# Layer-3 attention's first keys and queries prepared one stage earlier, its row scores first, three dense products before and in its first batch, and the output stored by chunk

## The chip, the cores and the metric

The kernel runs on one core of a Trainium2 chip. The metric is the device time of one execution in microseconds, and lower is better. Three runs of the kernel before took 2995.62, 2998.90 and 3001.24 us, so the median is 2998.9 us.

## The reference

A network of four layers works on 16 sequences of 256 tokens with 128 features, all in float32. Each layer is a macaron: half a feed-forward network, attention, and half of the same feed-forward network again, each on the layer norm of x and added to x. The change touches layer 3 alone:

```python
x = x + 0.5 * ffn(layernorm(x));  x = x + attn(layernorm(x));  x = x + 0.5 * ffn(layernorm(x))

def attn(x, W_q, W_k, W_v, W_o):             # 16 heads of 8 features
    q, k, v = heads(x @ W_q.T), heads(x @ W_k.T), heads(x @ W_v.T)
    s = einsum('bhqd,bhkd->bhqk', q, k) / sqrt(8)
    return merge(einsum('bhqk,bhkd->bhqd', softmax(s), v)) @ W_o.T

def ffn(x, ...):                             # 128 -> 512 -> 512 -> 512 -> 128
    h = silu(lin(x, w1)) * lin(x, w2)
    h = gelu(lin(h, h1));  h = gelu(lin(h, h2))
    return lin(h, w3)
```

## The kernel before, in words

The program is a row of stages, one after the other, with a barrier of all engines at the start of each (`Stage.ready`). x stays in SBUF throughout, in `fields`, as 32 tiles of 128 tokens. A chunk is 4 tiles (`CT`), that is 512 tokens (`CW`) or two sequences, and there are 8 chunks. Each stage has a program for SP (which issues DMAs in order), GpSimd, VectorE, ScalarE and TensorE, and each engine runs its program strictly in order; semaphores tie them together. `sig.past(n)` is the count that a signal has after its n-th event, plus the credit that it starts with. The layer norm has helpers: `ln_scales_dve` (L143 to 155) forms mean and variance from sums kept with x, `ln_scales_pool` (L161) takes the power, `ln_dve` (L180) normalises a chunk into `xn`, `ln_pe` (L190) transposes it into the one PSUM bank `tp`, and `ln_act` (L196) copies that to `xnt`. `new_sums_dve` (L203) forms the sums of a new chunk of x.

`l3_ffn` runs twice, with first=True ahead of the attention and first=False behind it. In each chunk (`body`) TensorE makes eight products of the hidden layer (L2834); ScalarE takes silu (L2767) and VectorE multiplies (L2746). Then come two layers h1 and h2 (`layer`), each in seven products of half size (L2788) instead of eight, by a scheme of sums and differences: VectorE forms the sums t1 to t4 (L2713 to 2721) and combines each product from its PSUM bank as soon as it is there (L2724 to 2738), ScalarE copies the first product (L2772) and takes gelu (L2775). In the end TensorE makes the output product (L2847), VectorE adds it to x (L2752) and forms the new sums (L203). Chunks 0 to 5 run in a hardware loop; chunks 6 and 7 are written out, and c is a Python integer there. SP has no program in this stage.

`l3_attn` handles a batch (one sequence) in 16 steps of two heads each. The scores are computed twice. `row_scores` (L3205) gives queries by keys, of which VectorE takes the maximum of each row (`largest`, L3052). The maxima are split into three bfloat16 parts (`split_maxima`, L3057 to 3063), transposed (`turn_maxima`, L3212), copied (`keep_nm`, L3137) and put by three small DMAs (`place_nm`, L2975) into three extra rows of the query tile `qx`. `key_scores` (L3221) then gives keys by queries with the maximum already taken off, ScalarE takes the exponential (L3133), and `values` (L3233) multiplies with V. Row scores run ahead: 16 steps of batch 0 and `LEAD` = 8 steps of batch 1 come ahead of the main loop, and the loop makes those of later batches between its own steps. The main loop's first instruction on TensorE is a row-score step that waits for `nm_moved`.

Keys and queries are float32 values held as three bfloat16 parts each, laid out in 72 rows (`kx`, `qx`), which are filled through DRAM. For each chunk TensorE makes two projections (`project`, L3191), ScalarE copies them to `proj` (`keep`, L3128), a split makes the three parts, SP stores them to `k_dram` and `q_dram` (`store`, L2954 and 2957) and loads them once per batch in the order that the scores need (`load`, L2965 and 2968: one transfer of 576 KB and three of 192 KB). For chunks 0 and 1 VectorE makes the split in the stage's start (L3034 to 3040), for the others GpSimd in the loop (L3018 to 3024). Order at the stage's start, on each queue:

- SP: four weight loads (L2946), the ones (L2979), store(0,0), load(0,0,0), load(0,0,1), store(1,1), load(1,1,0), place_nm(0,0,0).
- TensorE: four weight transposes (L3261), `ln_pe` 0, K and Q projection of chunk 0, `ln_pe` 1, K and Q projection of chunk 1, V projection of chunk 0 (L3195), 16 row-score steps of batch 0, 8 of batch 1 with the transposes of the maxima behind the second, main loop.
- VectorE: constants (L3080 to 3082), layer-norm scales, `ln_dve` 0 and 1, four splits, the copy of V (`keep_v`, L3045), 16 maxima, `split_maxima`, 8 maxima, main loop.
- ScalarE: four weight copies (L3151, L3153), then for each of two chunks `ln_act` and two `keep`, `keep_nm`, main loop.

The last stage, `end`, waits at its barrier and stores all of x with one DMA (L3399).

## Time and profile before

| | |
|---|---|
| Median of three runs | 2998.9 us |
| The profiled execution's own time | 3000.47 us |
| Its span | 2998.3 us |
| Mean granted clock of TensorE | 0.851 of full speed |
| Layer-3 feed-forward, first run of it | 2076 to 2365 us of the span |
| Layer-3 attention | 2367 to 2698 us |
| Layer-3 feed-forward, second run of it | 2699 to 2989 us |
| Output | 2989.5 to 2998.3 us |

The profile shows one execution. Engines are PE (TensorE's matmuls), PEld (its weight loads, which overlap them), DVE (VectorE), ACT (ScalarE), POOL (GpSimd) and SP. L12 is line 12 of the kernel. In the timeline each line has the start, the duration of the whole group, the engine, the line, the operation, output<-inputs, the count, and in brackets the engine's idle time before it with what ended it. The table of stretches gives, for each stretch of the span, its length, then busy time and count of PE, PEld, DVE, ACT and POOL in this order, PEclk, the DMA engines' share and GB/s. PEclk is the TensorE clock that the throttle granted, as a share of full speed: 1.00 is 2.4 GHz, 0.50 is 1.2 GHz. Ends of matmuls are modelled, so a busy PE is not necessarily PE at its peak. A float32 product of 512 columns is two matmul instructions.

### The profile page before, as it was taken

Reading aid. Unit: us, or ns where it says so; the run is one execution under the profiler, and the core shown is the slowest. Engines: PE = TensorE matmul, PEld = TensorE weight load, DVE = VectorE, ACT = ScalarE, POOL = GpSimd, SP = SyncE. Lnnn points to the kernel's source line nnn. Section 1 sums busy time; section 2 is a strip of 40 time slices with the busy share of each in tenths; the row PEclk is TensorE's granted clock in tenths of the full one; section 3 lists DMA queues with packets and bytes.
Section 4 is the critical chain, followed back from the end, with each engine's and each line's share of the span. In section 5 each row is a group of like instructions: output and inputs, shape, how many; then the busy total and the mean of one; then the engine's idle time right before and its main releaser. Section 6 shows DMA issues by size and latency. Waiting matters only on the chain. (4 is left out here: it accounts for less than half of the span.)

```text
span 2998.3 us, 46339 instructions
## 1 busy us (share of the span) xinstructions
PE 2306.7 (77%) x14088; PEld 1668.0 (56%) x14089; DVE 1753.8 (58%) x4313; ACT 1064.7 (36%) x2478; POOL 850.1 (28%) x770
## 2 busy tenths in 40 slices
PE   4979959767376740675999982575999799989998
PEld 3645546447354720563666651464888545547877
DVE  5758957563576359821343348833565578765565
ACT  1433324431144110453444422353333246663332
POOL 2535425437313730673000010574000112201000
PEclk9989959865596555897999986798999779999999
DMA  6110011336514675454000017364000133310000
GB/s 207 39 59 1 1 40 41 101 139 143 144 34 153 144 211 71 92 119 117 1 1 0 1 40 143 77 122 99 1 0 0 36 96 89 87 43 1 0 0 29
DMA packets 274629, 204.04 MB, mean 68 GB/s; under 512 B 102432, under 2 KB 253453, under 8 KB 271405
## 3 DMA queue, kind: packets, MB, share of 16 engines
q1 hardware_dynamic: 240301, 168.05, 20.2%
q0 software_dynamic: 34176, 34.09, 7.0%
q8 instruction: 79, 1.29, 0.2%
q14 instruction: 73, 0.60, 0.1%
HBM read 136.20 MB, written 64.91 MB: 67 GB/s over the span
## 5 line engine op out<-in xcount | busy, mean ns | idle before, releaser
L161 POOL TENSOR_TENSOR fields<-ln_t,power 128x4 f32<-128x4 f32 x96 | 98.3, 1050 | 590.9 <-DVE ln_t L154 590.9
L3052 DVE TENSOR_REDUCE s_mx<-s_sa 128x2 f32<-128x512 f32 x256 | 166.2, 686 | 57.8 <-PE s_sa L3205 56.7
L3133 ACT ACTIVATE s_e<-s_sc 128x512 f32<-128x512 f32 x256 | 149.7, 600 | 99.6 <-PE s_sc L3221 96.7
L2788 PE MATMUL s_z<-s_t,s_mix_h 128*128 128x256 f32 x768 | 171.0, 379 | 0.0
L1996 POOL DMA_INDIRECT acc_dram<-s_yo,s_to_i x96 | 152.4, 1588 | 45.8 <-issue 27.0
L1984 POOL DMA_INDIRECT s_xg<-rows_dram,s_from_i x96 | 94.6, 985 | 223.0 <-DVE s_to_i L2117 195.0
L2788 PEld LDWEIGHTS s_z<-s_t,s_mix_h 128*128 128x128 f32 x768 | 146.0, 190 | 19.7
L190 PE MATMUL s_tp<-ident,xn 128*128 128x128 f32 x224 | 46.4, 344 | 133.8 <-DVE xn L180 132.0
L2406 DVE TENSOR_SCALAR s_den<-s_kn 128x8 f32<-128x8 f32 x64 | 10.3, 161 | 209.0 <-PE s_kn L2567 209.0
L3205 PE MATMUL s_sa<-s_kx,s_qx 72*128 72x256 bf16 x512 | 109.4, 300 | 27.1 <-DMA s_qx<-q_dram 15.0
L2301 PE MATMUL s_hu<-s_xgt,s_w 128*128 128x128 f32 x768 | 118.1, 300 | 7.9 <-issue 6.0
L2834 PE MATMUL s_z<-xnt,s_wt_w 128*128 128x512 f32 x256 | 116.8, 610 | 1.5 <-ACT xnt L196 1.5
L190 PEld LDWEIGHTS s_tp<-ident,xn 128*128 128x128 f32 x224 | 34.2, 183 | 147.5 <-DVE xn L180 133.7
L2396 POOL TENSOR_TENSOR s_rd<-s_rv,s_power 128x2 f32<-128x2 f32 x16 | 11.1, 697 | 369.5 <-DVE s_rv L2430 369.5
L1251 POOL DMA_INDIRECT acc_dram<-s_yo,s_to_i x64 | 101.7, 1588 | 30.6 <-issue 17.6
L2206 ACT ACTIVATE s_h<-s_hu,s_b 128x128 f32<-128x128 f32 x384 | 109.1, 375 | 1.2 <-PE s_hu L2301 1.2
L2301 PEld LDWEIGHTS s_hu<-s_xgt,s_w 128*128 128x128 f32 x768 | 99.3, 202 | 15.4 <-issue 9.4
L425 POOL DMA_INDIRECT y_dram<-s_xg,s_to_ids x78 | 76.7, 983 | 109.6 <-DVE s_xg L583 109.6
L2311 PE MATMUL s_lp<-s_w,s_h 128*128 128x128 f32 x768 | 106.2, 283 | 1.8 <-ACT s_h L2206 1.7
L3221 PE MATMUL s_sc<-s_qx,s_kx 75*128 75x256 bf16 x512 | 103.0, 285 | 0.9 <-DMA s_qx<-s_nm 0.5
L415 POOL DMA_INDIRECT s_xg<-x_dram,s_ids x78 | 75.5, 968 | 99.2 <-DVE s_ids L548 72.5
L2311 PEld LDWEIGHTS s_lp<-s_w,s_h 128*128 128x128 f32 x768 | 96.4, 197 | 3.5 <-ACT s_h L2206 3.5
(516 smaller groups left out, 6105.0 us busy)
## 6 DMA issues: line engine op xcount, KB each, us to landing
s_w<-in_L_ffn_W_dram SPq DMA_DIRECT2D x96, 256.0 KB, 3.0
acc_dram<-s_zero SPq DMA_DIRECT2D x32, 512.0 KB, 5.8
s_kx<-k_dram SPq DMA_DIRECT2D x16, 576.0 KB
s_qx<-q_dram SPq DMA_DIRECT2D x48, 192.0 KB
fields<-acc_dram SPq DMA_DIRECT2D x16, 512.0 KB, 7.5
table_dram<-s_table_rows SPq DMA_DIRECT2D x2, 3136.0 KB, 9.2
s_wg<-in_L_ffn_w_gate_dram SPq DMA_DIRECT2D x64, 96.0 KB, 2.1
s_wu<-in_L_ffn_w_up_dram SPq DMA_DIRECT2D x64, 96.0 KB, 2.2
```

The source lines that it names most:

```text
L161: pool.tensor_tensor(core.rstd[:, tiles], core.ln_t[:, 2, tiles], core.power[:, 0:CT], ALU.pow).then_inc(s.scale_ready.sem, 1)
L1251: pool.indirect_dma_start(sums, bass.IndirectOffsetOnAxis(ap=to_i[:, n:n + 1], axis=0), yo[:, n % RING, :], None, compute_op=ALU.add).then ...
L1996: pool.indirect_dma_start(sums, bass.IndirectOffsetOnAxis(ap=to_i[:, n:n + 1], axis=0), yo[:, n % RING, :], None, compute_op=ALU.add).then ...
L2206: last = act.activation(h[:, u, j, :], hu[:, u, j * P:(j + 1) * P], ACT.Gelu, bias=b1[:, j, n:n + 1])
L2301: last = pe.matmul(hu[:, u, j * P:(j + 1) * P], w1[:, n % RING, j, :], xgt[:, u, :], start=True, stop=True)
L2311: pe.matmul(lp[:, u, j * P:(j + 1) * P], h[:, u, j, :], w2_flat[:, first:first + P], start=j == 0, stop=False)
L2788: last = pe.matmul(bank(n)[:, o, :], weights[:, f, o * P:(o + 1) * P], src[:, f, :], start=f == 0, stop=f == HALF - 1)
L2834: pe.matmul(z[:, (2 * f + half) % 4, :], wt[m][:, 0, f * P:(f + 1) * P], core.xnt[:, u, :], start=True, stop=True).then_inc(up_done.sem, 1)
L3052: dve.tensor_reduce(mx[:, i, t, 2 * pairs:2 * pairs + 2], sa[:, n % 2, :, :], AX.X, ALU.max).then_inc(max_done.sem, 1)
L3133: act.activation(e[:, n % RING, :, :], sc[:, n % 2, :, :], ACT.Exp).then_inc(exp_done.sem, 1)
L3205: last = pe.matmul(sa[:, n % 2, a, :], qx[0:ROWS, slot, h, t * P:(t + 1) * P], kx[0:ROWS, slot, h, :], start=True, stop=True)
L3221: last = pe.matmul(sc[:, n % 2, a, :], kx[:, slot, h + a, k * P:(k + 1) * P], qx[:, slot, h + a, :], start=True, stop=True)
```

## The change

In `l3_ffn` with first=True, chunks 6 and 7 also prepare keys and queries of chunks 0 and 1 for the attention (a = 0 in chunk 6, a = 1 in chunk 7): layer norm from x, transposes, two projections, three parts and their stores. The helper `early(c, k, at)` on each engine is called at places inside `layer`, where k is the layer and `at` the place. The work area is `all_xn`, free in this stage, and the bank `tp`. In `l3_attn` SP begins with the load of batch 0, and TensorE with its row scores; weight transposes, `ln_pe` and the V projection stand between row-score steps 10 and 15. `keep_v` stands behind `split_maxima`. `warm()` is a product of 512 columns whose result nobody reads, twice ahead of the main loop and once at step 1 of batch 0. In the last stage each chunk of x is stored as soon as it is added up, and the sums L203 are left out there. The stage `end` is gone.

```diff
@@ l3_ffn, SP @@
+        if first:
+            @block.sync
+            def _(sp):
+                for n, m in enumerate(("W_k", "W_q")):
+                    sp.dma_start(raw_a[n], w[f"L3_attn_{m}"]).then_inc(aw_loaded.sem, 16)
+                for a in range(EARLY):
+                    for n in range(2):
+                        sp.wait_ge(a_split_done.sem, a_split_done.past(2 * a + n))
+                        for i in range(2):
...
+                                sp.dma_start(core.k_dram[2 * a + i].rearrange("a d h t -> (d h) a t"), cut).then_inc(a_stored[0].sem, 16)
+                            else:
+                                for k in range(TERMS):
+                                    sp.dma_start(core.q_dram[2 * a + i, :, k, :, :], cut[:, k, :]).then_inc(a_stored[1].sem, 16)
+                sp.wait_ge(a_stored[0].sem, 32 * EARLY)
+                sp.wait_ge(a_stored[1].sem, 32 * TERMS * EARLY)
+        if not first:
...
+                for c in range(CHUNKS):
+                    tiles = slice(c * CT, (c + 1) * CT)
+                    sp.wait_ge(x_added.sem, x_added.past(c))
+                    sp.dma_start(out_rows[:, tiles, :], core.x[:, tiles, :]).then_inc(out_stored.sem, 16)
+                sp.wait_ge(out_stored.sem, 16 * CHUNKS)
@@ l3_ffn, VectorE @@
+            def early_left(a, n):
+                dve.wait_ge(a_first_cut.sem, a_first_cut.past(2 * a + n))
+                dve.scalar_tensor_tensor(left[n], s.tp[:, 0, :], SCALE if n else 1.0, parts[:, n, 0, :],
+                                         ALU.mult, ALU.subtract).then_inc(a_left_ready.sem, 1)
+            def early_last(a, n):
+                dve.wait_ge(a_second_cut.sem, a_second_cut.past(2 * a + n))
+                dve.tensor_tensor(parts[:, n, 2, :], left[n], parts[:, n, 1, :], ALU.subtract).then_inc(a_split_done.sem, 1)
+            def early(c, k, at):
...
+                if a == 0 and k == 0:
+                    if at == 0:
+                        early_scales()
+                    if at == 3:
+                        early_normal(0, range(2))
+                    if at == 4:
+                        early_normal(0, range(2, CT))
+                if (a, k) in ((0, 1), (1, 0)):
+                    if at == 2:
+                        early_left(a, 0)
+                    if at == 4:
+                        early_last(a, 0)
+                    if at == 5:
+                        early_left(a, 1)
+                if a == 0 and k == 1 and at == 6:
+                    early_last(0, 1)
+                if a == 1 and k == 1 and at == 0:
+                    early_last(1, 1)
...
             def body(c, u, more=True):
                 if more:
                     ln_dve(dve, core, s, c + 1, 1 - u)
+                elif first:
+                    early_normal(1)
...
-                dve.wait_ge(x_added.sem, x_added.past(c))
-                new_sums_dve(dve, core, c)
+                if first:
+                    dve.wait_ge(x_added.sem, x_added.past(c))
+                    new_sums_dve(dve, core, c)
@@ l3_ffn, ScalarE @@
+            def early_cut(a, n):
+                act.wait_ge(a_projected.sem, a_projected.past(2 * a + n))
+                if a:
+                    act.wait_ge(a_stored[n].sem, (32, 32 * TERMS)[n] * a)
+                act.activation(parts[:, n, 0, :], s.tp[:, 0, :], ACT.Copy, scale=SCALE if n else 1.0).then_inc(a_first_cut.sem, 1)
+            def early_cut2(a, n):
+                act.wait_ge(a_left_ready.sem, a_left_ready.past(2 * a + n))
+                act.activation(parts[:, n, 1, :], left[n], ACT.Copy).then_inc(a_second_cut.sem, 1)
...
+                if (a, k) in ((0, 1), (1, 0)):
+                    if at == 1:
+                        early_cut(a, 0)
+                    if at == 2:
+                        early_cut2(a, 0)
+                    if at == 3:
+                        early_cut(a, 1)
+                    if at == 4:
+                        early_cut2(a, 1)
@@ l3_ffn, TensorE @@
+            def early_project(a, n):
+                if n:
+                    pe.wait_ge(a_left_ready.sem, a_left_ready.past(2 * a))
+                else:
+                    pe.wait_ge(a_xnt_ready.sem, a_xnt_ready.past(a))
+                pe.matmul(s.tp[:, 0, :], wt_a[n], xta, start=True, stop=True).then_inc(a_projected.sem, 1)
...
                 product(held.quarter(m, 0, 1), b21, 1)
+                early(c, k, 1)
...
                 product(s2, t2, 4)
+                early(c, k, 2)
...
                 product(held.quarter(m, 1, 1), t4, 0)
+                early(c, k, 5)
                 pe.wait_ge(taken.sem, taken.past(now))
                 product(s4, b22, 1)
+                early(c, k, 6)
@@ l3_attn, SP @@
-            for m in names:
-                sp.dma_start(raw[m][:, :], w[f"L3_attn_{m}"]).then_inc(w_loaded.sem, 16)
...
+            load(0, 0, 0, False)
+            for m in names:
+                sp.dma_start(raw[m][:, :], w[f"L3_attn_{m}"]).then_inc(w_loaded.sem, 16)
+            load(0, 0, 1, False)
             sp.wait_ge(ones_ready.sem, 1)
...
-            store(0, 0)
-            load(0, 0, 0, False)
-            load(0, 0, 1, False)
-            store(1, 1)
             load(1, 1, 0, False)
             place_nm(0, 0, 0)
@@ l3_attn, VectorE @@
-            dve.memset(ones[:, :], 1.0).then_inc(ones_ready.sem, 1)
-            dve.memset(m3[:, :, :, TERMS:, :], 0.0)
-            dve.tensor_copy(ident_b[:, :], core.ident[:, :]).then_inc(ident_ready.sem, 1)
             ln_scales_dve(dve, core, s)
             ln_dve(dve, core, s, 0, 0)
             ln_dve(dve, core, s, 1, 1)
-            split(0, 0)
-            split(0, 1)
-            split(1, 0)
-            split(1, 1)
-            dve.wait_ge(v_clear.sem, 2)
-            keep_v(0, 0)
+            dve.memset(ones[:, :], 1.0).then_inc(ones_ready.sem, 1)
+            dve.memset(m3[:, :, :, TERMS:, :], 0.0)
+            dve.tensor_copy(ident_b[:, :], core.ident[:, :]).then_inc(ident_ready.sem, 1)
             for n in range(STEPS):
                 largest(0, 0, n)
             split_maxima(0)
+            dve.wait_ge(v_clear.sem, 2)
+            keep_v(0, 0)
@@ l3_attn, TensorE @@
+            def warm():
+                pe.matmul(pj[:, :], wt["W_v"][:, :], core.xnt[:, 0, :], start=True, stop=True)
...
             pe.wait_ge(kq_loaded[0].sem, 64)
             for n in range(STEPS):
                 row_scores(0, 0, n)
+                if n == T_FIRST:
+                    pe.wait_ge(w_loaded.sem, 16 * len(names))
...
+                if n == T_FIRST + 1:
+                    ln_pe(pe, core, s, 0, 0)
+                if n == T_FIRST + 3:
+                    ln_pe(pe, core, s, 1, 1)
+                if n == T_FIRST + 4:
+                    pe.wait_ge(w_kept.sem, 1)
+                    project_v(0, 0)
...
+            pe.wait_ge(v_kept.sem, v_kept.past(0))
+            warm()
+            warm()
             pe.wait_ge(ones_loaded.sem, 16)
-            pe.wait_ge(v_kept.sem, v_kept.past(0))
...
                             turn_maxima(b + 1, 1 - i)
+                        if n == 1 and not prev:
+                            warm()
                         key_scores(b, slot, n)
```

T_FIRST is 10. The credits of `pj_kept` and `parts_stored` are raised by what chunks 0 and 1 gave before, and the counts that wait for them shift by 2 * EARLY.

## Rows read from the trace of the kernel before

**Rows 1.** The table of stretches: length, busy time of each engine, PEclk, DMA share, GB/s.

```profile
2298.00:2334.00 36.00, 36.00 (x167) 28.59 (x166) 20.38 (x34) 12.26 (x18) 0.00 (x0) 1.00 0.00 1
...
2371.00:2399.00 28.00, 12.58 (x28) 5.48 (x27) 14.22 (x25) 4.37 (x10) 10.09 (x10) 0.50 0.35 88
...
2406.00:2424.00 18.00, 13.23 (x50) 4.84 (x50) 13.35 (x27) 3.58 (x6) 0.00 (x0) 0.50 0.62 151
...
2424.00:2440.00 16.00, 16.00 (x94) 7.13 (x94) 8.07 (x15) 7.48 (x14) 0.00 (x0) 0.50 0.01 3
...
2456.00:2488.00 32.00, 30.43 (x294) 17.69 (x286) 25.33 (x60) 21.48 (x41) 8.74 (x8) 1.00 0.40 96
...
2610.00:2620.00 10.00, 10.00 (x73) 5.08 (x71) 5.75 (x11) 5.96 (x12) 2.40 (x3) 0.80 0.17 25
...
2704.00:2716.00 12.00, 11.51 (x28) 5.93 (x29) 3.77 (x6) 4.63 (x7) 4.37 (x5) 0.77 0.00 1
```

**Rows 2.** Timeline of the attention stage's start: start us, us, engine, line, operation [idle before].

```profile
2366.94 0.34 SPq L2946 DMA_DIRECT2D s_raw_W_q<-in_L_attn_W_q_dram  x1
...
2371.25 1.12 PE L190 MATMUL s_tp<-ident,xn 128*128 128x128 f32 x4
...
2385.16 2.07 PE L3195 MATMUL s_pj<-s_wt_W_v,xnt 128*128 128x128 f32 x8 [0.69 <-ACT s_proj L3128]
...
2389.58 0.80 SPq L2965 DMA_DIRECT2D s_kx<-k_dram  x1
...
2391.97 0.88 DVE L3045 COPY s_vz<-s_pj 128x128 f32<-128x128 f32 x4
...
2398.94 1.04 PE L3205 MATMUL s_sa<-s_kx,s_qx 72*128 72x256 bf16 x4 [11.71 <-DMA s_qx<-q_dram]
```

**Rows 3.** Timeline of the first maxima and the loop's start.

```profile
2399.59 11.04 DVE L3052 TENSOR_REDUCE s_mx<-s_sa 128x2 f32<-128x512 f32 x16 [6.74 <-PE s_sa L3205]
...
2411.62 5.46 DVE L3052 TENSOR_REDUCE s_mx<-s_sa 128x2 f32<-128x512 f32 x8
...
2412.60 2.60 SPq L2975 DMA_DIRECT2D s_qx<-s_nm  x3
...
2419.29 0.59 PE L3205 MATMUL s_sa<-s_kx,s_qx 72*128 72x256 bf16 x2 [2.94 <-DMA s_qx<-s_nm]
```

**Rows 4.** End of the program on the timeline; transfers' sizes and time to landing.

```profile
2987.33 0.69 DVE L2752 TENSOR_TENSOR fields<-fields,s_y 128x512 f32<-128x512 f32 x1 [2.93 <-PE s_y L2847]
...
2988.05 0.87 DVE L203 BATCH_NORM_STATS2 fields<-fields 128x6 f32<-128x128 f32 x4
...
out_dram<-fields SPq DMA_DIRECT2D x1, 2048.0 KB, 8.4
...
s_raw_W_q<-in_L_attn_W_q_dram SPq DMA_DIRECT2D x1, 64.0 KB, 1.8
```

**Rows 5.** Timeline of the first feed-forward stage, chunks 6 and 7.

```profile
2308.35 0.69 DVE L2729 TENSOR_TENSOR s_u<-s_u,s_z 128x512 f32<-128x512 f32 x1 [1.04 <-PE s_z L2788]
...
2329.03 7.03 PE L2834 MATMUL s_z<-xnt,s_wt_w 128*128 128x512 f32 x16
```

**Rows 6.** Timeline of the first batch: value products and the first K projection.

```profile
2426.86 1.08 PE L3233 MATMUL s_ob<-s_e,s_vz 128*32 128x256 f32 x8
...
2429.70 1.08 PE L3233 MATMUL s_ob<-s_e,s_vz 128*32 128x256 f32 x8
...
2439.82 1.92 PE L3191 MATMUL s_pj<-xnt,s_wt_W_k 128*128 128x512 f32 x2
...
2442.95 0.76 PE L3233 MATMUL s_ob<-s_e,s_vz 128*32 128x256 f32 x8
```

**Rows 7.** Timeline of later batches: value products, and a wait for a load.

```profile
2493.13 0.64 PE L3233 MATMUL s_ob<-s_e,s_vz 128*32 128x256 f32 x8
...
2494.68 0.64 PE L3233 MATMUL s_ob<-s_e,s_vz 128*32 128x256 f32 x8
...
2606.04 0.39 PE L3205 MATMUL s_sa<-s_kx,s_qx 72*128 72x256 bf16 x2 [1.96 <-DMA s_qx<-q_dram]
```

More of the change, by code:

```diff
@@ L2689, in _ @@
             ln_scales_pool(pool, core, s)
+            if first:
+                pool.wait_ge(a_var_ready.sem, 1)
+                for c in range(EARLY):
+                    tiles = slice(c * CT, (c + 1) * CT)
+                    pool.tensor_tensor(core.rstd[:, tiles], core.ln_t[:, 2, tiles], core.power[:, 0:CT],
+                                       ALU.pow).then_inc(a_scale_ready.sem, 1)
         @block.vector
@@ L2704, in _, with early_scales @@
                     dve.tensor_tensor(s4, a12, s2, ALU.subtract).then_inc(mixed.sem, 1)
+            def early_scales():
+                tiles = slice(0, EARLY * CT)
+                me, mo = core.sums[:, tiles, 1], core.sums[:, tiles, 4]
+                t0, t1, t2 = (core.ln_t[:, i, tiles] for i in range(3))
+                dve.tensor_tensor(t0, me, mo, ALU.add)
+                dve.tensor_tensor(t1, me, mo, ALU.subtract)
+                dve.tensor_tensor(t2, core.sums[:, tiles, 2], core.sums[:, tiles, 5], ALU.add)
+                dve.drain()
+                dve.tensor_scalar(core.mean[:, tiles], t0, 0.5, None, ALU.mult)
+                dve.tensor_tensor(t1, t1, t1, ALU.mult)
+                dve.tensor_scalar(t2, t2, 1.0 / D, 1e-5, ALU.mult, ALU.add)
+                dve.drain()
+                dve.scalar_tensor_tensor(t2, t1, 0.25, t2, ALU.mult, ALU.add).then_inc(a_var_ready.sem, 1)
@@ new lines, in early_normal @@
+            def early_normal(a, tiles=range(CT)):
+                dve.wait_ge(a_scale_ready.sem, a_scale_ready.past(a))
+                if a:
+                    dve.wait_ge(a_turned.sem, a_turned.past(a - 1))
+                for j in tiles:
+                    t = a * CT + j
+                    last = dve.tensor_scalar(xa[:, j, :], core.x[:, t, :], core.mean[:, t:t + 1], core.rstd[:, t:t + 1],
+                                             ALU.subtract, ALU.mult)
+                if CT - 1 in tiles:
+                    last.then_inc(a_xn_ready.sem, 1)
@@ L3422, in build @@
             l3_ffn(core, held, False)
-        end(core)
 def kernel(**inputs):
```

161 lines of the change are left out of this document (108 added, 53 removed).

## The prediction

> **What bounds the kernel now.** I read the stages first, in the table of stretches. In the first Layer-3 feed-forward stage TensorE is busy 36.00 of 36 us at the full clock, VectorE 20.4 and ScalarE 12.3 [rows 1]: every product put there lengthens it, vector and scalar work need not. The start of the attention stage is the opposite: TensorE is busy 12.58 of 28 us from 2371 to 2399, and its granted clock is 0.50, the 1.2 GHz level, from there through 2440, even in 2424 to 2440 where it is busy 16.00 of 16 us. The same loop later runs at 1.00 [rows 1].
>
> The timeline then says what the start waits for. The first DMA is issued at 2366.94; call that t = 0. Weights, projections, splits in three parts, the store to DRAM and the load back follow each other; the load is issued at t = 22.6 and the first row scores run at t = 32.0, after 11.71 us idle for that DMA [rows 2]. Then VectorE sets the pace: 16 maxima take 11.04 us, 8 more 5.46 us, and the main loop begins at 2419.29, t = 52.35, behind the three transfers of the maxima [rows 3]. At the end of the program the last addition starts at 2987.33; the sums for a layer norm that nobody reads, a barrier and one 2048 KB store, 8.4 us to landing, are all exposed [rows 4].
>
> **The change, part by part.** Durations are those of one execution: 3000.47 us, span 2998.3 us, 2.2 us around it. The median of the runs shown is 2998.9, 1.6 us lower; I subtract my sum from the median as well.
>
> *Early keys and queries, in the feed-forward stage.* TensorE gets four projections of 512 columns, two matmuls each: 16 such matmuls take 7.03 us [rows 5], so 0.88 us each and 3.5 us. It gets 10 transposes; four took 1.12 us at the half clock [rows 2], so 0.14 us each at full clock and 1.4 us. That is 4.9 us on a full engine; I take **+5.0**. VectorE gets eight normalisations, four subtractions and four last parts of 0.69 us, and seven small operations for the scales, about 9 us over some 60 us; ScalarE eight cuts and four copies, about 7 us; GpSimd two small powers. Cover: VectorE idles 1.04 us ahead of most reads of a product [rows 5] and 2.93 us ahead of the last addition [rows 4], and the added pieces are put behind such reads one at a time. The tightest place is the end of the first layer of chunk 7: one 0.69 us subtraction stands ahead of the next layer's first sum, about the slack that the third product there leaves. If instead each of the four projections exposed its copy and its subtraction (0.6 + 0.69 us), the cost would be 10; the floor is 3.5, projections alone. SP, empty in this stage before, issues two weight loads and 16 stores. The last ones are released early in chunk 7's second layer, with most of a layer and the output products still to run, more than the 9.4 us that a whole load took [rows 2]; they should not hold the barrier.
>
> *Row scores first.* SP now issues load(0,0,0) at t = 0, ahead of the four weight loads, the other loads, the ones and the maxima. The transfer that let scores start 9.36 us after its issue [rows 2] does so at t = 9.4. Bounds: 7.5, if the second load behind it took some of the bandwidth; 12, if the weights and two more loads disturb it more. Its cover is gone, for nothing else is ready: PE waits for it alone. The 16 maxima take 11.7 us from there (2398.94 to 2410.63). Between steps 10 and 14 PE now does the four weight transposes, two turns of xn and the V projection: 1.1 + 1.1 + 1.1 + 2.07 us at the half clock [rows 2]. PE needs 0.43 us for a step where VectorE needs 0.69 and runs at most two steps ahead; followed step by step, VectorE starves for 0.2, 0.8 and 2.4 us, so +3.4 (bounds 1 and 5.4). Maxima done: t = 24.5. Splitting them takes 1.0 us (2410.63 to 2411.62), the V copy that now stands behind it 0.9 [rows 2], the 8 maxima of the next batch 5.5; PE's last row scores need the sixth of them and end at t = 31.1. The transfers of the maxima start at t = 26.4 and take 2.6 us to issue; before, the scores waited 4.1 us beyond that [rows 3], with a load issued just ahead in the same queue. Now the loads stand long before them; with the 1.8 us of a small transfer [rows 4] they land at 30.8, at worst 33.1. Two dense products at the half clock, 1.76 us each (twice 0.88), end at t = 34.6 and cover both. So the loop starts at 34.6 and not at 52.35: **-17.8** (bounds -14 and -21).
>
> *Three dense products.* The first 16 steps took 23.66 us, 2419.29 to 2442.95; two steps take 2.84 us at the half clock, 1.55 at the full one [rows 6, 7]. Eight pairs at 1.55, the norm transposes and one K projection give about 14; the 16 maxima with their normalisation want 12.9 on VectorE; I take 15. So a full clock from the first step is worth 8.7. Against it, the third product costs 0.9 to 1.0 in the loop, and I allow 1.2 for a rise inside the first pairs. **-6.5**, bounds +1.8 (no rise) and -8.
>
> That the clock rises is the uncertain step. In 2424 to 2440 a busy engine stayed at 0.50, and the next short durations stand right behind the 1.92 us K projection of 2439.82 [rows 1, 6]; the next feed-forward stage starts cold with such products and has a mean of 0.77 within 12 us [rows 1]. Dense products raise it, row and key scores alone did not. But single projections with pauses, 2371 to 2399, did not either. The Trainium skill ("TensorE: Matmul & The Clock Gate", Part 1) says that sustained matmul activity releases the throttle and an idle stretch brings it back. By that rule 2424 to 2440 should have been fast, and the three products would be a mere cost, with the time of rival (a); the trace disagrees with it, 16.00 us busy at 0.50.
>
> *Output by chunk.* Seven stores of 256 KB land beside chunks 1 to 7. The last follows the last addition, done at 2988.02. Between 64 KB in 1.8 us and 2048 KB in 8.4 us [rows 4] lies 2.4 for 256 KB; with 0.15 of wake and the 0.36 that the span had after landing it ends at 2990.9 for 2998.3: **-7.3** (bounds -6.5 and -7.7). The sums that go with it cost nothing in the other chunks, where TensorE is full.
>
> Sum: 5.0 - 17.8 - 6.5 - 7.3 = -26.6. The profiled execution would be 2973.9, the median **2972**.
>
> **Rivals.** (a) *The clock does not rise before the first K projection.* For it: the cold projections with pauses, and scores that hold nothing up. The third product costs 1.8 and nothing comes back: 5.0 - 17.8 + 1.8 - 7.3 = -18.3, time 2981. (b) *The faster loop start runs into the loads.* The loop has such a wait: 1.96 us for a load at 2606.04, and a clock of 0.80 in the ten microseconds after it [rows 1, 7], some 4 us together. If the ring of stores and loads, now entered sooner, makes two more of these, 2980. Against it: later rounds already run at this pace. (c) *The feed-forward stage loses its clock.* The new handshakes are the first pauses that TensorE would have in chunks 6 and 7. Where they bring 1.2 GHz, the work takes twice as long: x us of full-clock work cost x. It decides from about 33 of the 72 us on (26.6 gained, 6 of margin); the whole second chunk, 36 us, gives 3008. Against it: each projection waits for work that is finished a product earlier, and the clock was 1.00 throughout.
>
> **Numbers.** Forecast 0.63, with 2966 to 2977 as its own range; (a) 0.20; (b) 0.11; (c) 0.06. The range reaches over (a) and (b) with the bounds of the load: 2963 to 2984. A measurement of this kernel tells about 0.2%, 6 us, from no change. Forecast, (a) and (b) are all beyond it; of (c) most is slower, some cancels, and a late load together with (a) could come near: faster 0.92, same 0.03, slower 0.05.
>
> **What would show it.** Feed-forward chunks 6 and 7 some 2.5 us longer each, clock 1.00; first row scores 9 to 10 us after the stage's first DMA; the loop's first step near t = 35; the first eight pairs at 1.5 to 2 us each; the end 3 us behind the last addition. The forecast is wrong if the granted clock of the first batch stays at 0.50, if the first load lands after t = 12, or if the feed-forward chunks grow by more than 5 us each.

## The result and the profile after

| | before | changed |
|---|---|---|
| Median, same comparison | 3000.07 us (6 executions, 2995.62 to 3011.46) | 2966.11 us (6 executions, 2959.86 to 2969.40) |
| Ratio | | 0.9878, interval [0.9859, 0.9896] |
| Span of the profiled execution | 2998.3 us | 2965.7 us |
| Mean granted clock | 0.851 | 0.858 |

The changed kernel is 34.0 us faster by the medians. The forecast was 26.6 us less, 2972 with a range of 2963 to 2984. A second set of six executions gave 2972.80 us for the same kernel; all twelve together have a median of 2968.5.

The table of stretches of the changed kernel, columns as in [rows 1], around the places that those rows show of before:

```profile
2301.00:2337.00 36.00, 36.00 (x173) 28.84 (x171) 24.12 (x47) 14.44 (x24) 1.99 (x2) 1.00 0.05 14
2371.00:2399.00 28.00, 13.75 (x70) 8.11 (x68) 15.32 (x39) 1.98 (x6) 11.73 (x11) 0.63 0.62 127
2399.00:2409.00 10.00, 6.83 (x28) 2.76 (x27) 7.21 (x18) 1.67 (x2) 0.00 (x0) 0.83 0.50 120
2408.40:2424.00 15.60, 15.09 (x136) 8.05 (x135) 12.06 (x25) 10.35 (x20) 0.13 (x1) 1.00 0.15 34
2424.00:2440.00 16.00, 15.57 (x152) 9.09 (x149) 13.44 (x31) 11.21 (x22) 8.60 (x8) 1.00 0.19 52
2456.00:2488.00 32.00, 31.05 (x302) 18.07 (x300) 25.97 (x61) 22.48 (x43) 8.74 (x8) 1.00 0.40 101
...
2610.00:2620.00 10.00, 8.92 (x93) 5.43 (x91) 7.98 (x19) 6.84 (x14) 0.00 (x0) 1.00 0.77 183
```

The feed-forward stage still has a full TensorE at the full clock, with four more microseconds of VectorE in 36. Ahead of the main loop the clock still has means of 0.62 and 0.83. From the loop's start, 2408.40, it is 1.00, where the loop before began at 0.50 and stayed there through 2440 [rows 1].

The timeline of the attention stage's start in the changed kernel (start us, us, engine, line, operation, idle time before), against [rows 2, 3, 6]:

```profile
2375.90 0.84 SPq L3170 DMA_DIRECT2D s_kx<-k_dram  x1
2376.79 1.34 SPq L3173 DMA_DIRECT2D s_qx<-q_dram  x3
...
2385.83 1.03 PE L3393 MATMUL s_sa<-s_kx,s_qx 72*128 72x256 bf16 x4 [13.14 <-DMA s_qx<-q_dram]
2386.47 7.66 DVE L3245 TENSOR_REDUCE s_mx<-s_sa 128x2 f32<-128x512 f32 x11 [5.34 <-PE s_sa L3393]
...
2394.47 1.06 PE L190 MATMUL s_tp<-ident,xn 128*128 128x128 f32 x4
...
2397.62 1.08 PE L3383 MATMUL s_pj<-s_wt_W_v,xnt 128*128 128x128 f32 x8
...
2401.50 1.87 SPq L3180 DMA_DIRECT2D s_qx<-s_nm  x3
...
2405.55 3.05 PE L3398 MATMUL s_pj<-xnt,s_wt_W_v 128*128 128x512 f32 x4
2408.44 0.38 PE L3393 MATMUL s_sa<-s_kx,s_qx 72*128 72x256 bf16 x2
...
2409.10 1.02 PE L3398 MATMUL s_pj<-xnt,s_wt_W_v 128*128 128x512 f32 x2
...
2411.90 0.64 PE L3424 MATMUL s_ob<-s_e,s_vz 128*32 128x256 f32 x8
```

Counted from the stage's first DMA, at 2375.90, the row scores begin at t = 9.9 (32.0 before) and the loop at t = 32.5 (52.35 before). The first value burst takes 0.64 us, where those of the first batch took 1.08 [rows 6].

The end of the changed kernel on its timeline, against [rows 4]:

```profile
2962.08 0.69 DVE L2876 TENSOR_TENSOR fields<-fields,s_y 128x512 f32<-128x512 f32 x1 [2.93 <-PE s_y L3053]
2962.79 0.37 SPq L2737 DMA_DIRECT2D out_dram<-fields  x1
```

and the store in the list of DMA issues on its page (size, us to landing):

```profile
out_dram<-fields SPq DMA_DIRECT2D x8, 256.0 KB, 2.3
```

**Where the time went.** I put the same marks on every profile. The *feed-forward* part runs from the stage's first layer-norm operation (L146 in the kernel before) to its last addition. *Load* runs from the attention stage's first DMA to the first row scores, *maxima* from there to the first operation of `split_maxima`, and *wait* from there to the loop's first step. *First batch* runs to the seventh value burst (2442.95 in [rows 6]), and *rest* from there to the attention's last addition to x. *End* runs from the program's last addition to the end of the span.

| kernel | feed-forward | load | maxima | wait | first batch | rest | end | span |
|---|---|---|---|---|---|---|---|---|
| before | 287.36 | 32.00 | 11.79 | 8.56 | 23.66 | 254.09 | 10.97 | 2998.3 |
| changed | 293.10 | 9.93 | 13.91 | 8.70 | 14.50 | 248.65 | 3.62 | 2965.7 |

Between these two executions the differences are +5.74 in the feed-forward stage, -19.81 in load, maxima and wait, -9.16 in the first batch, -5.44 in the rest and -7.35 at the end. The code ahead of the stage, which is the same, took 3.09 us more (2079.62 for 2076.53 us), and the gaps between the stages and the last feed-forward stage differ by 0.33 together. The sum is -32.6, the difference of the spans. Two of these entries are not the change's: the 3.09 and, as the experiments show, the 5.44.

Part of the 5.74 isn't either. The feed-forward stage starts at the lower clock in every profile, and for how long differs. Its first 16 us in the kernel before and in the changed one:

```profile
2076.50:2092.50 16.00, 11.68 (x33) 6.38 (x34) 12.12 (x29) 4.87 (x7) 9.80 (x8) 0.74 0.01 2
...
2079.60:2095.60 16.00, 11.69 (x27) 5.71 (x28) 11.04 (x27) 4.56 (x7) 9.80 (x8) 0.66 0.04 10
```

I take 16 times what PEclk lacks to 1.00 in these first 16 us off the length of the stage (before: 287.36 - 16 * 0.26 = 283.2; changed: 293.10 - 16 * 0.34 = 287.7). What is left is 283.1 to 283.2 us in the three profiles with the old stage and 287.6 to 287.8 in the ten with the new one and single projections. So the early keys and queries cost 4.5 us there, and 1.3 of the 5.74 are the clock at the stage's start.

### The profile page after: what moved, and what is told of

It reads as the page before. It is cut to its first block and busy times, and to the rows that moved or that the text cites. A ratio compares the mean times of both kernels' runs of the same rounds, so it can differ in the third digit from the quotient of the medians.

```text
span 2965.7 us, 46268 instructions
## 1 busy us (share of the span) xinstructions
PE 2292.0 (77%) x14104; PEld 1665.7 (56%) x14105; DVE 1740.3 (59%) x4288; ACT 1068.0 (36%) x2486; POOL 852.3 (29%) x772
## 3 DMA queue, kind: packets, MB, share of 16 engines
q8 instruction: 80, 1.31, 0.2%
## 5 line engine op out<-in xcount | busy, mean ns | idle before, releaser
L3393 PE MATMUL s_sa<-s_kx,s_qx 72*128 72x256 bf16 x512 | 102.5, 284 | 24.9 <-DMA s_qx<-q_dram 14.2
L196 ACT ACTIVATE xnt<-s_tp 128x512 f32<-128x512 f32 x56 | 33.5, 598 | 186.6 <-PE s_tp L190 186.6
```

The lines of the kernel that those rows point to most:

```text
L3393: last = pe.matmul(sa[:, n % 2, a, :], qx[0:ROWS, slot, h, t * P:(t + 1) * P], kx[0:ROWS, slot, h, :], start=True, stop=True)
```

## The experiments

Twelve kernels ran, in three sets of four, each set with its own executions of before: median 2998.84 us (14 executions) for before_again, before_dense, no_dense and no_third; 3001.25 (11) for after_again, one_store, double_projection and load_alone; 3000.46 (11) for no_two, queries_first, early_load and both. A gain below is the difference to the median of the same set. The table holds the marks of each kernel's one profiled execution; *start to loop* is load, maxima and wait together. *Clock loss* is a sum over the rest of the loop: it is cut into stretches of 8 us (the last 10 us or more left out), and each adds 8 times what its PEclk lacks to 1.00. The last column has TensorE's waits of 1.0 us or more for a DMA in that part.

| kernel | median | gain | feed-forward | load | start to loop | first batch | rest | clock loss | end | waits for a DMA |
|---|---|---|---|---|---|---|---|---|---|---|
| before | 3000.07 | | 287.36 | 32.00 | 52.35 | 23.66 | 254.09 | 5.3 | 10.97 | 1.12, 1.96, 1.13 |
| before_again | 2996.90 | | 288.49 | 33.10 | 54.12 | 23.52 | 249.05 | 0.0 | 11.90 | 1.13 |
| before_dense | 2990.76 | 8.1 | 287.60 | 33.02 | 53.70 | 14.49 | 259.22 | 8.6 | 10.95 | 1.96, 1.07, 1.32 |
| changed | 2966.11 | 34.0 | 293.10 | 9.93 | 32.54 | 14.50 | 248.65 | 0.0 | 3.62 | 1.08 |
| after_again | 2972.80 | 28.5 | 292.92 | 9.51 | 33.16 | 15.21 | 260.45 | 12.0 | 3.69 | 1.31, 1.72, 1.02 |
| no_dense | 2974.85 | 24.0 | 292.16 | 9.56 | 29.48 | 22.90 | 256.83 | 8.6 | 3.60 | 1.02, 1.47, 1.39 |
| no_two | 2962.64 | 37.8 | 291.85 | 9.83 | 29.48 | 16.45 | 247.61 | 0.0 | 3.68 | none |
| no_third | 2972.25 | 26.6 | 292.71 | 9.70 | 32.20 | 14.49 | 252.77 | 3.4 | 3.64 | 1.38, 1.18 |
| one_store | 2979.62 | 21.6 | 292.97 | 9.82 | 32.41 | 14.48 | 258.14 | 11.9 | 11.18 | 1.01, 1.53 |
| double_projection | 2971.37 | 29.9 | 296.53 | 9.33 | 32.57 | 14.50 | 252.73 | 3.4 | 3.66 | 3.40 |
| load_alone | 2970.39 | 30.9 | 292.31 | 9.34 | 34.54 | 15.86 | 257.60 | 10.2 | 3.71 | 1.06, 1.85 |
| queries_first | 2967.96 | 32.5 | 292.62 | 9.13 | 32.84 | 15.24 | 254.73 | 6.9 | 3.29 | 1.60, 1.56 |
| early_load | 2962.41 | 38.1 | 293.37 | 0.23 | 26.70 | 15.25 | 254.28 | 5.1 | 3.35 | 1.16, 1.09, 2.01 |
| both | 2975.29 | 25.2 | 293.23 | 0.23 | 26.63 | 15.20 | 253.05 | 5.1 | 3.75 | 1.32, 1.45 |

### The kernel before, once more

No edit. Expected:

> The kernel before, unchanged, for a second trace. Disputed is the stretch of the attention loop behind its first batch: 254.1 us in the first trace of before, 248.6 us in the trace of the changed kernel, which the prediction had at no difference. Theory A (the waits for loads and the low clock after them come and go from one execution to the next): this trace gives something other than 254, about 249 to 255, and its waits for the loads fall in other places. Theory B (the faster start removes them): 254 again, with the same wait near the middle of the loop, within 0.5 us.

One execution, 2996.9 us. The rest of its loop took 249.05 us, not 254.09. So the 5.44 us that the changed kernel seemed to save there lie within what one kernel does from one execution to the next.

### The dense products, all and one at a time

no_dense takes all three out; no_third takes out the one inside the loop, no_two the pair ahead of it; before_dense puts all three into the kernel before. Nobody reads these products, so leaving them out changes nothing that is computed.

```diff
-            warm()
-            warm()
...
-                        if n == 1 and not prev:
-                            warm()
```

> The changed kernel without its three dense products. Theory A (they bring the full clock to the first batch): the loop's first step comes some 2.7 us earlier, held by the row scores instead of the products, the first batch takes 22 to 24 us at a granted clock near 0.5 where the changed kernel takes 14.5 us, and the whole is 5 to 7 us slower than the changed kernel, about 2972. Theory B (the work now put between the row scores, above all the V projection during which the clock rose in the changed kernel's trace, does it alone): the first batch stays near 14 us and the whole is 3 us faster, about 2963.

> The changed kernel without the third dense product, the one at step 1 of batch 0. Theory A (two are enough, the third is a cost): first batch 0.9 us shorter at the full clock, the whole 0 to 1 us faster. Theory B (the clock falls again without it): first batch 20 us or more in some or all executions, the whole up to 8 us slower.

> The kernel before with nothing but the three dense products, at the same places. Theory A (they act by themselves): they end about 0.6 us later than the maxima's transfers, the first batch takes about 14.5 us instead of 23.7, and the whole is 8 to 9 us faster than before. Theory B (they act only together with the denser row scores of the changed kernel): the first batch stays near 23 us and the whole is 1 to 2 us slower than before.

> The changed kernel without the two dense products ahead of the loop; the one behind the first row scores of the next chunk, inside the loop, stays (nobody reads any of them). If it is these two that bring the clock back for the loop's first scores: the first seven value bursts take about 22.9 us, as with all three taken out, instead of 14.5, or somewhat less if the third product, some 10 us into the loop, raises the clock there (then about 18), and the prologue is some 3 us shorter, so that the kernel is 3 to 6 us slower than the changed one. If the clock would have risen by the work of the stage anyway: 14.5 us for the first bursts and 3 us faster than the changed kernel.

The stretch of no_dense that holds its first batch, in the columns of [rows 1]:

```profile
2404.00:2427.00 23.00, 22.75 (x121) 10.90 (x121) 12.64 (x25) 9.73 (x18) 0.00 (x0) 0.52 0.19 49
```

and that of before_dense:

```profile
2421.30:2435.90 14.60, 14.02 (x126) 7.50 (x126) 11.44 (x24) 9.31 (x18) 0.00 (x0) 1.00 0.26 57
```

With no dense product TensorE is busy 22.75 of 23 us and stays at the lower level, although the early keys and queries, the early load and all else of the change are there. With the products alone, in the kernel before, the first batch takes 14.49 us at 1.00 and the kernel gains 8.1 us (ratio 0.9970, interval [0.9957, 0.9983]). So the products are what raises the clock for the first batch, with the old start and with the new one.

no_third has the same first batch as the changed kernel, 14.49 us for 14.50: once the clock is up, the third product costs nothing. TensorE has room for it there: without it it is busy 13.40 of the 14.60 us. The medians can't confirm so small an effect: no_third has 2972.25 us, 3.8 above the changed kernel's twelve executions, and its six spread from 2965.16 to 2978.36. no_two shows that the third product isn't idle where it stands alone. Its timeline at the loop's start (TensorE only):

```profile
2398.63 0.58 PE L3393 MATMUL s_sa<-s_kx,s_qx 72*128 72x256 bf16 x2
2399.01 0.63 PE L3412 MATMUL s_sc<-s_qx,s_kx 75*128 75x256 bf16 x2
2399.43 0.63 PE L3393 MATMUL s_sa<-s_kx,s_qx 72*128 72x256 bf16 x2
2399.86 1.91 PE L3398 MATMUL s_pj<-xnt,s_wt_W_v 128*128 128x512 f32 x2
...
2402.42 1.04 PE L190 MATMUL s_tp<-ident,xn 128*128 128x128 f32 x4
2403.27 0.40 PE L3412 MATMUL s_sc<-s_qx,s_kx 75*128 75x256 bf16 x2
...
2404.05 0.64 PE L3424 MATMUL s_ob<-s_e,s_vz 128*32 128x256 f32 x8
```

Key scores of 0.63 us before the product have become 0.40 at 2403.27, 1.5 us behind its end. Without the pair the loop starts earlier, t = 29.48 for 32.54 (29.48 in no_dense too), and the first batch takes 16.45 us. From the first DMA to the seventh burst that is 45.93 us, for 47.04 with all three, 46.69 with the pair alone and 52.38 with none. The one product inside the loop does all that the three do, and the pair's own price, 3.1 us of the start, is saved. My expectation that no_two would be 3 to 6 us slower was wrong: a first batch of 18 us, which it allowed for, and a start 3 us shorter come to 0.5 us slower, and not to 3 to 6.

### The changed kernel, once more

No edit; in the set with the next three.

> The changed kernel, unchanged, again, as the measure for the three others and for the loop behind the first batch, which has taken 248.6 to 259.2 us in six traces whatever the kernel. Theory A (that stretch varies by waits for loads and low clock behind them, which no part of the change steers): 2966 again within 3 us, the stretch anywhere in 248 to 260, all other marks within 0.7 us of the first trace. Theory B (the changed kernel is steadily free of these waits): the stretch 248 to 249 again.

All marks up to the loop lie within 0.7 us of the first profile, and the first batch takes 0.7 us more. The clock rose later there, some 2 us into the loop. The loop's first 3 us:

```profile
2408.30:2411.30 3.00, 3.00 (x14) 1.83 (x13) 2.31 (x6) 0.65 (x2) 0.00 (x0) 0.66 0.58 109
```

Of the ten profiles with the pair, five have first batches of 14.48 to 14.50 us; in the other five (after_again, load_alone, queries_first, early_load, both) the first 3 us have a mean of 0.51 to 0.66, and the batch takes 15.20 to 15.86.

The rest of the loop differs far more: 260.45 us for 248.65, with a span of 2978.3. The median of 2972.80 lies outside the 3 us around 2966 that I had expected. The table of stretches:

```profile
2520.30:2536.30 16.00, 15.03 (x110) 7.92 (x111) 9.21 (x17) 8.70 (x17) 3.43 (x4) 0.79 0.35 65
2536.30:2544.30 8.00, 7.53 (x75) 5.17 (x74) 7.05 (x20) 4.55 (x10) 5.32 (x5) 1.00 0.23 65
2544.30:2562.30 18.00, 16.77 (x123) 8.97 (x120) 11.25 (x25) 9.55 (x18) 0.00 (x0) 0.72 0.57 135
```

and its timeline at the two waits behind which the first losses of this loop stand, from 2442 (outside the stretches shown) and from 2521:

```profile
2442.02 0.39 PE L3393 MATMUL s_sa<-s_kx,s_qx 72*128 72x256 bf16 x2 [1.31 <-DMA s_qx<-s_nm]
...
2521.27 0.39 PE L3393 MATMUL s_sa<-s_kx,s_qx 72*128 72x256 bf16 x2 [1.72 <-DMA s_qx<-q_dram]
```

TensorE waits 1.3 or 1.7 us for a transfer, and a stretch below the full clock follows: 16 us at 0.79 behind the second wait, which are 3.4 us lost. This is the pattern of rival (b).

### One store at the end

The changed kernel with the old `end` stage and its sums; the feed-forward stage stores nothing.

```diff
-                    sp.wait_ge(x_added.sem, x_added.past(c))
-                    sp.dma_start(out_rows[:, tiles, :], core.x[:, tiles, :]).then_inc(out_stored.sem, 16)
...
+            sp.dma_start(core.out.rearrange("b (n p) d -> p (b n) d", p=P), core.x[:, :, :]).then_inc(out_stored.sem, 16)
+            sp.wait_ge(out_stored.sem, 16)
```

> The changed kernel with the output stored as before: one store of all of x in a stage of its own, and the sums formed again in the last stage. Theory A (the part acts at the end alone): from the last addition to the end 11.0 us and not 3.6, everything else the same, the whole 7.3 us slower than the changed kernel. Theory B (stores and missing sums also act within the stage): the last feed-forward stage itself differs from 288.4 us by over 0.5 us.

Its end, on the timeline:

```profile
2967.62 0.69 DVE L2864 TENSOR_TENSOR fields<-fields,s_y 128x512 f32<-128x512 f32 x1 [2.93 <-PE s_y L3040]
2968.35 0.87 DVE L203 BATCH_NORM_STATS2 fields<-fields 128x6 f32<-128x128 f32 x4
...
2969.83 0.41 SPq L3577 DMA_DIRECT2D out_dram<-fields  x1
```

11.18 us for 3.69 in after_again, so 7.5 us; the medians differ by 6.8 (2979.62 for 2972.80). The feed-forward stage of the end keeps its length, 288.7 us for 288.5: the seven stores beside it are free, and the sums that fell away there give nothing back.

### Each early projection twice

```diff
+                pe.matmul(s.tp[:, 0, :], wt_a[n], xta, start=True, stop=True)
                 pe.matmul(s.tp[:, 0, :], wt_a[n], xta, start=True, stop=True).then_inc(a_projected.sem, 1)
```

> The changed kernel with each of the four early projections made twice into the same place. Theory A (TensorE is full there, so that all it gets is paid): four more products of 512 columns, 0.86 us each, make the first Layer-3 feed-forward stage 3.4 us longer, 293.1 to 296.5. Theory B (part of the 5.7 us that the stage grew is waiting between engines, and TensorE has room there): it grows by less than 2 us. The whole 3.4 us slower, or 0 to 2.

The first product of each pair does the same work once more. The stage took 296.53 us, 291.1 without the clock's loss in its first 16 us (PEclk 0.66), where the ten profiles with single projections have 287.6 to 287.8. So four more projections cost 3.4 us, 0.86 each, which is TensorE's own time for them: TensorE is the limit there. The median doesn't show it, 2971.37 us for 2972.80 in after_again; the scatter of the executions is larger.

### The first load alone in the queue

SP waits for the first load before it issues anything else.

```diff
             load(0, 0, 0, False)
+            sp.wait_ge(kq_loaded[0].sem, 64)
             for m in names:
```

> The changed kernel, with SP waiting for the load of batch 0 to land before it issues the weights, the second load, the ones and the third load. Theory A (the first load shares the DMA engines with what is issued behind it): it lands after some 7.5 us and not 9.9, the loop starts 2.4 us earlier, since the weights (2 us) and the second load are still in time for steps 10 and 16, and the whole is 2 us faster. Theory B (the first load is served in order and has the engines to itself already): it lands at 9.5 to 9.9 again and nothing gains; if the second load then comes late, up to 2 us slower.

The first scores began 9.34 us after the first DMA, alone in the queue, and 9.13 to 9.93 us in the eight profiles with the other loads behind it. Those loads take nothing from it that this scatter would let one see. The Trainium skill ("DMA: Bandwidth & Descriptors", the section "Queues, rings and completion order") says that each DMA engine takes the descriptors of one queue in order; the 9.34 against 9.13 to 9.93 agrees.

What was held back came late, and the loop began at t = 34.54 for 32.54. The row scores of the second batch waited only 0.34 us for their load. The loop's first step waited longer, TensorE idle for 2.57 us behind the pair:

```profile
2407.31 3.00 PE L3399 MATMUL s_pj<-xnt,s_wt_W_v 128*128 128x512 f32 x4
2412.88 0.53 PE L3394 MATMUL s_sa<-s_kx,s_qx 72*128 72x256 bf16 x2 [2.57 <-issue]
```

The profile names no cause for that idle time, but this step waits for the three transfers of the maxima, issued from 2403.26 on, and the view of the tile `s_nm` has for them

```profile
DMA to landing us min/median/max: 4.2/4.5/8.2
```

for 1.9/1.9/2.0 in no_third. The last was issued at 2404.54, so it landed at about 2412.8. Why it took 8.2 us is open.

### Queries ahead of keys in the loop

In the loop the queries are projected, split, stored and loaded ahead of the keys, and their load is issued ahead of the transfers of the maxima.

```diff
-                pe.matmul(pj[:, :], wt["W_q" if n else "W_k"][:, :], core.xnt[:, u, :], start=True, stop=True).then_inc(projected.sem, 1)
+                pe.matmul(pj[:, :], wt["W_k" if n else "W_q"][:, :], core.xnt[:, u, :], start=True, stop=True).then_inc(projected.sem, 1)
...
                     store(c + 2, u)
+                    load_q(c + 2, u, 0)
                 if after:
                     place_nm(2 * c + 2, 2 * (1 - u), 0)
                 if after > 1:
-                    load(c + 2, u, 0)
+                    load_k(c + 2, u, 0)
```

> The changed kernel with the queries projected, split and stored before the keys, and the load of the queries issued ahead of the transfers of the row maxima, that of the keys behind them. My theory: in the loop the row scores of a new slot wait for the queries' load, by 0.3 to 3.4 us, and the rest of the attention loop is 248.7 us in an execution without a late one and up to 260.5 us with late ones and the stretches at 0.5 clock that follow. If so, the waits of TensorE for the queries' load are gone or under 0.3 us each, the rest of the loop stands at 248 to 252 us, and the median is about 4 us under the changed kernel's, 2966 us by the one or 2964 by the other. First rival: the waits move to the keys' load, now last, and nothing is gained (within 2 us of the changed kernel). Second rival: the transfers of the row maxima now stand behind the queries' load and come late, so that the scores of the next chunk wait for them: slower by 1 us or more for each chunk, 5 us and up in all.

The summed waits of TensorE in the loop of queries_first (us in total, times, the longest):

```profile
PE s_sa L3401 <- DVE s_mx L3253: 4.4, 15, 0.5
PE s_sa L3401 <- DMA s_qx<-s_nm: 4.4, 5, 1.6
```

and of the changed kernel:

```profile
PE s_sa L3393 <- DVE s_mx L3245: 4.4, 15, 0.5
PE s_sa L3393 <- DMA s_qx<-s_nm: 2.2, 3, 0.8
PE s_sa L3393 <- DMA s_qx<-q_dram: 1.1, 1, 1.1
```

The waits for the load of queries are gone, as expected, but those for the transfers of the maxima became longer, 1.60 and 1.56 us, and each stands ahead of a stretch below 1.00. The rest was 254.73 us, outside the expected 248 to 252; the median, 2967.96, is the changed kernel's (2968.5 over its twelve executions). What happened is the second rival's mechanism, the transfers of the maxima late behind the queries' load, at a smaller price than its 5 us and up. The three longest waits for these transfers in the loops of all fourteen profiles are those of the two kernels with this order (1.60 and 1.56 here, 1.45 in both). The keys' load, the first rival's candidate, appears in no wait.

### The first load one stage earlier, and both

early_load gives the first batch's keys and queries tiles of their own and loads them while the feed-forward stage still runs. The attention stage begins with row scores.

```diff
@@ l3_ffn, SP, behind the stores of a = 0 @@
+                        sp.wait_ge(a_stored[0].sem, 32)
+                        sp.wait_ge(a_stored[1].sem, 32 * TERMS)
+                        sp.dma_start(slot0[0][0:72, :, :].rearrange("r h t -> r (h t)"),
+                                     core.k_dram[0].rearrange("a d h t -> (a d) (h t)").unsqueeze(1).to_broadcast([24, 3, 16 * N])).then_inc(a_loaded.sem, 16)
...
@@ l3_attn, SP @@
-            load(0, 0, 0, False)
@@ l3_attn, VectorE @@
+            largest(0, 0, 0)
             ln_dve(dve, core, s, 0, 0)
```

> The changed kernel with the first keys and queries also loaded in the feed-forward stage (in tiles of their own, kept over both stages), so that the row scores can begin as the attention stage does. My theory: what is left of the prologue, 32.5 us, is 9.5 us of the first load, 13.9 us of row scores and maxima, and 8.9 us of the transfers of the maxima and dense products. With the load gone the row scores begin within 1 us, but the second slot's row scores, and the fold that follows the first maxima, still wait for nothing but VectorE: the loop starts at about 24 to 27 us instead of 32.5, and the kernel is 5 to 8 us faster than the changed one, 2960 to 2964 us. Rival: the second slot's load, which follows right behind, becomes the wait (it cannot land before 8 to 10 us into the stage, and its own maxima take 5.5 us more), and the weights of the projections come late to TensorE; then the loop starts at 30 us or later and 0 to 2.5 us are gained. Other rival: the waits inserted into the feed-forward stage cost there what they save here.

> The last two changes together. If they are independent, the gain is the sum of the two, 9 to 12 us under the changed kernel's time, about 2957 to 2960 us. If the loop is set by one wait alone that both act on, the gain is no more than the larger of the two.

The start of early_load's attention stage on its timeline (its first DMA is issued at 2371.89):

```profile
2372.12 0.60 PE L3407 MATMUL s_sa<-s_kx,s_qx 72*128 72x256 bf16 x4 [3.46 <-PEq L80]
2373.97 0.61 PE L3407 MATMUL s_sa<-s_kx,s_qx 72*128 72x256 bf16 x2 [1.26 <-DVE s_mx L3258]
2377.83 1.21 PE L3407 MATMUL s_sa<-s_kx,s_qx 72*128 72x256 bf16 x4 [3.25 <-DVE s_mx L3258]
```

The scores begin 0.23 us after the first DMA. VectorE then becomes what they wait for: the layer norm stands between its first and its second maximum, 3.25 us of idle TensorE. So of the 9.7 us of load that went, 5.8 are gained at the loop's start, t = 26.70 for 32.54. The feed-forward stage did not grow (293.37 us, 287.6 without its clock loss). The median of 2962.41 is 6.1 us under the changed kernel's 2968.5, as expected, and its four executions are the narrowest of all (2960.78 to 2963.54).

Both together did not add up: 2975.29 us, from 2962.47 to 2984.54. Only its fastest execution has a profile, and that one has the marks of early_load within 0.2 us but for the rest. Where the slower ones lose up to 22 us more isn't seen.

## Why the prediction was right

The mechanism forecast for each of the four parts happened. 2966.11 us lies 6 us under the forecast and 0.1 us inside its own range. The start and the first batch gave more than they were put at. Term by term:

- **Early keys and queries, +5.0.** Measured +5.7 in the first pair of profiles, of which 1.3 is the clock at the stage's start, and +4.5 without that. The price of a projection was 0.88 us and 0.86 was measured; the ten transposes then cost about 1.0, for 1.4. The list of waits of the changed kernel from 2300 to 2372 has none of TensorE's, so no handshake was exposed, and the clock was 1.00 there: the bound of 10 and rival (c) fall.
- **First load, t = 9.4.** 9.9, and 9.1 to 9.9 in the repeats. Neither bound was needed.
- **Maxima with the inserted work, 15.1 us from the first scores (11.7 and 3.4).** 13.9. The mis-sized term is the inserted work, 2.1 us more than before instead of 3.4. It was priced at the lower clock throughout, with the V projection at 2.07 us [rows 2]. It took 1.08: the clock had risen by 2397.62, behind row scores, weight transposes and turns of xn one after the other. Which of them raised it no run takes apart. It fell again in the pauses that followed (0.83 in 2399 to 2409, above), before the pair.
- **Loop start, t = 34.6.** 32.5. The load came 0.5 us later than put, the maxima and the inserted work took 1.2 less, the way from there to the pair 5.8 us instead of 6.6, and the pair 2.9 instead of 3.5 up to the loop's first step. One step of the prediction's reasoning was wrong here: it had the dense products "cover" the transfers of the maxima, landing at t = 30.8 or later. They landed within 2.0 us of their issue in no_third, at about t = 28.5, and the pair began at t = 29.4. So the pair covers nothing, and without it the loop starts 3.1 us earlier (no_two, no_dense).
- **First batch, 15 us.** 14.5. The gain is 9.2 us where the three products were put at 6.5. The failing part of that term is the 1.0 us for the third product, which no_third shows to be 0; the 1.2 us for a late rise did not happen in this profile, and cost 0.7 to 1.4 us in five of ten.
- **Output, -7.3.** -7.35, and 7.5 between after_again and one_store. 256 KB land in 2.3 us, for an interpolated 2.4.

Together the changed parts gave 5.74 - 19.81 - 9.16 - 7.35 = -30.6 in the profiles, 4 us more than the forecast's -26.6: 2.0 from the loop's start, 2.7 from the first batch, less 0.7 in the feed-forward stage. The medians differ by 34.0; the other 3.4 us belong to no part of the change. The second six executions gave 28.5, so how far the median of the first six lies from the forecast is in part chance.

**The rivals.** (a), no rise of the clock, is what no_dense shows in part: a first batch of 22.90 us. It was rightly the strongest rival, since scores and value products alone did not raise the clock, and it fails because the dense products do. That disagreement with the Trainium skill ("TensorE: Matmul & The Clock Gate", Part 1), whose rule is that sustained matmul activity releases the throttle, stands: 22.75 us of 23 busy at a PEclk of 0.52 in no_dense. (b), new waits for loads, exists as a pattern but not as a price of the change: clock losses of 5.3, 0.0 and 8.6 us stand in the three profiles with the old start, and of 0.0 to 12.0 in those with the new one. Whether the earlier loop start adds a microsecond or two on average can't be told from one profile of each kernel.

## What to carry to other kernels

Read the granted clock of a stage beside its busy time: here one float32 product of 512 columns that nobody reads, 1.9 us at most, saved 6.5 us (45.93 us for 52.38, no_two and no_dense), so try one before several, and count what each costs in the place where it stands. Work moved out of a serial start into a stage with a full TensorE cost its TensorE time there, 4.5 us for the 20 that the start gave back. And where executions of one kernel differ by up to 20 us, compare stage by stage: the totals of one pair of profiles put 5.4 us into the change's account that were not its own.

## What the runs showed that I had not expected

**The rest of the loop is one number plus its clock losses.** In the table above the rest goes from 247.61 to 260.45 us. Less the clock loss it is between 246.2 and 250.7 in all fourteen profiles, old and new (before: 254.09 - 5.3 = 248.8; after_again: 260.45 - 12.0 = 248.4). So the scatter between executions of this kernel lies in TensorE's clock. All 19 stretches below 1.00 in that part of the loop stand behind a wait of TensorE for a transfer, the shortest 1.01 us (one_store) and the longest 3.40 (double_projection). The reverse does not hold: 9 of the 28 waits in the table have none behind them, among them 1.08 in the changed kernel, 1.13 in before_again and 1.47 in no_dense. double_projection's longest, from its waits in the loop:

```profile
PE s_sa L3394 <- DMA s_qx<-q_dram: 4.3, 4, 3.4
```

and the two stretches of its table around it:

```profile
2608.00:2616.00 8.00, 6.53 (x68) 3.72 (x66) 6.60 (x16) 5.03 (x9) 0.00 (x0) 1.00 0.76 141
2616.00:2632.00 16.00, 14.08 (x112) 8.07 (x113) 9.16 (x16) 8.26 (x16) 0.00 (x0) 0.79 0.41 74
```

How long a stretch lasts isn't set by the wait either. In load_alone one wait of 1.85 us, which ended at 2623.46, stands ahead of the whole loss of 10.2 us:

```profile
2624.00:2646.00 22.00, 22.00 (x131) 11.85 (x130) 11.69 (x23) 9.67 (x18) 0.00 (x0) 0.53 0.19 39
```

TensorE is full there at the lower level, as in the first batch of no_dense. A dense product in such a place was not tried.

That the waits bring the clock down is the reading that fits; no run here removed them all. queries_first removed one kind and got another. Of the three profiles without a loss, no_two has no wait of 1.0 us, and the changed kernel and before_again have one each (1.08 and 1.13); what they did otherwise, with the same loop, stays open.

**Two versions beat the changed kernel's medians**, early_load (2962.41) and no_two (2962.64), by different means: an earlier load, and two products fewer. They were not tried together. And both, which holds all of early_load's gain at the start, had a median 12.9 us above early_load's; why is open.
